# Moving the second gate, two shared-expert steps and one column copy in the last layer of a fused four-layer kernel

## The reference

```python
def _L3_ffn_ref(x, centroids, gate_bias, wg_s, wu_s, wd_s, wg, wu, wd):
    def _swiglu(x, wg, wu, wd):
        return jax.nn.silu(x @ wg) * (x @ wu) @ wd
    shared = _swiglu(x, wg_s, wu_s, wd_s) * RATIO
    affinity = jax.nn.sigmoid(jnp.einsum('bsh,eh->bse', x, centroids))
    _, top_idx = jax.lax.top_k(affinity + gate_bias, K)
    top_aff = jnp.take_along_axis(affinity, top_idx, axis=-1)
    weights = top_aff / (top_aff.sum(-1, keepdims=True) + EPS)
    mask = (jax.nn.one_hot(top_idx, E, dtype=x.dtype) * weights[..., None]).sum(-2)
    routed = jnp.zeros_like(x)
    for e in range(E):
        routed = routed + mask[..., e:e + 1] * _swiglu(x, wg[e], wu[e], wd[e])
    return shared + routed
...
x = x + _L3_xattn_ref(_layernorm(x, axis=-1), ctx_2048, ...)
x = x + _L3_ffn_ref(_layernorm(x, axis=-1), ...)
```

## Time and profile before

| | |
|---|---|
| median of three runs | 1159.66 us (1155.91 to 1160.9) |
| the profiled execution | 1160.9 us |
| its span in the trace | 1159.6 us |
| mean granted clock of TensorE | 0.914 of full speed |
| busy, share of the span | PE 85%, PEld 68%, DVE 66%, ACT 55%, POOL 45% |

### The profile page before, as it was taken

One profiled execution on the slowest core, in us unless ns is written; L12 is line 12 of the kernel. 1 busy time (PEld: TensorE's weight loads), 2 busy tenths in 40 slices (PEclk: granted clock), 3 DMA queues, 4 the chain that ended last, 5 costly groups with the idle time before them and its releaser, 6 DMA issues. The chain is left out here.

```text
span 1159.6 us, 17917 instructions
## 1 busy us (share of the span) xinstructions
PE 985.5 (85%) x5740; PEld 787.3 (68%) x5740; DVE 760.7 (66%) x2019; ACT 633.7 (55%) x1824; POOL 525.5 (45%) x582
## 2 busy tenths in 40 slices
PE   4957998187997964689999999999999889997897
PEld 2453555045585754578988888889899768676685
DVE  3766222275666428878888888887877588677544
ACT  1431444002124335779797879888888745463253
POOL 1441587243554343334545454544443236352453
PEclk8877999688997985779999999999999899998999
DMA  9130698920002764010101010101000025004584
GB/s 392 42 124 21 176 220 210 251 60 1 1 1 92 259 220 177 25 60 2 60 1 61 1 60 2 60 1 60 1 23 2 1 93 159 1 1 177 185 311 159
DMA packets 57261, 108.84 MB, mean 94 GB/s; under 512 B 13840, under 2 KB 35216, under 8 KB 55248
## 3 DMA queue, kind: packets, MB, share of 16 engines
q1 hardware_dynamic: 47920, 89.71, 23.3%
q0 software_dynamic: 9248, 18.00, 6.0%
HBM read 79.19 MB, written 27.42 MB: 92 GB/s over the span
## 5 line engine op out<-in xcount | busy, mean ns | idle before, releaser
L2919 POOL TENSOR_TENSOR a_p<-a_p,a_tot 128x128 f32<-128x128 f32 x64 | 51.0, 816 | 207.8 <-DVE a_tot L2531 207.8
L200 PE MATMUL bank<-a_w_high,a_in 128*128 128x128 f32 (+1 forms) x512 | 125.9, 287 | 5.3 <-DVE a_in L2131 4.5
L200 PE MATMUL bank<-a_w_low,a_in 128*128 128x128 f32 (+1 forms) x512 | 121.9, 284 | 0.0
L200 PEld LDWEIGHTS bank<-a_w_high,a_in 128*128 128x128 f32 x512 | 100.4, 196 | 7.5 <-issue 4.0
L200 PEld LDWEIGHTS bank<-a_w_low,a_in 128*128 128x128 f32 x512 | 100.5, 196 | 0.0
L2582 DVE TENSOR_REDUCE a_top<-bank 128x2 f32<-128x512 f32 (+1 forms) x96 | 56.9, 601 | 32.2 <-PE bank L2384 19.7
L2089 POOL DMA_INDIRECT f_ys<-f_y,f_got x54 | 51.8, 960 | 53.4 <-ACT f_y L2058 52.8
L2753 ACT ACTIVATE a_qn<-bank,a_q_shift,a_q_rstd 128x128 f32<-128x128 f32 x128 | 48.4, 461 | 42.0 <-POOL a_q_shift L256 42.0
L2560 DVE TENSOR_SCALAR a_qn<-bank,a_qk_minus,a_qk_rstd 128x128 f32<-128x128 f32 x192 | 64.1, 403 | 5.5 <-POOL a_qk_rstd L253 2.8
L2384 PE MATMUL bank<-a_kt,a_qt 128*128 128x256 f32 x256 | 67.1, 408 | 0.0
L200 PE MATMUL bank<-a_proj_high,a_catq 128*128 128x256 f32 x256 | 63.9, 288 | 1.0 <-issue 1.0
(11 more groups left out here) (424 smaller groups left out, 3016.9 us busy)
## 6 DMA issues: line engine op xcount, KB each, us to landing
expert<-in_experts SPq DMA_DIRECT2D x49, 384.0 KB, 4.4
f_expert<-in_experts SPq DMA_DIRECT2D x31, 384.0 KB, 6.2
third_shelf<-in_groups SPq DMA_DIRECT2D x8, 1024.0 KB, 6.5
f_got<-f_xs SPq DMA_DIRECT2D x10, 516.0 KB, 8.1
f_got<-f_ys SPq DMA_DIRECT2D x8, 512.0 KB, 5.1
third_shelf<-in_groups SPq DMA_DIRECT2D x8, 512.0 KB, 4.2
f_xs<-blank_zero SPq DMA_DIRECT2D x1, 3999.0 KB, 20.6
l_expert<-in_experts SPq DMA_DIRECT2D x10, 384.0 KB, 8.0
```

Source lines behind the costliest of these rows:

```text
L200: ins = pe.matmul(out, lhs, rhs, start=start and n == 0, stop=stop and n == len(pairs) - 1, skip_group_check=shared)
L2919: g_.tensor_tensor(cross_probs(m, ti), cross_probs(m, ti), over(m.tot[n % 2][:, first:first + HPG], SC), ALU.mult).then_inc(*s["cross_weig ...
```

## The change

It has four parts, all in the last layer.

1. `SPARSE3` takes 4 tiles of tokens through the shared experts ahead of the routed tiles where it took 5. So 8 of the 16 steps run ahead and 8 behind (10 and 6 before). `summed`, which says after how many additions a group of x is complete, is written for the new count.
2. On TensorE the gate's product of the second half is written ahead of the counts of the first half (`logits_tensor(k, p, s4, 1)` ahead of `ranks(0)`). For layer 1 this changes nothing, since `ranks(0)` stands further up there.
3. On VectorE the copy and the limit of the second half's logits are written ahead of the slots of the first half (`limit_vector` ahead of `slots_vector`).
4. In the attention the copy of the first half's columns moves from ahead of the addition of tile 6 to ahead of that of tile 7.

```diff
@@ -1487,12 +1487,11 @@
     def summed(self, n):
-        return self.early // self.shared + TOP * (n + 1) + (
-            0 if self.early == self.steps else NT - self.early // self.shared - (2 if n < GROUPS // 2 else 0))
+        return self.early // self.shared + TOP * (n + 1) + (0 if self.early == self.steps else HALF // 2 if n < GROUPS // 2 else HALF)
...
-SPARSE3 = Sparse("f3", 1 + E0 + 1 + E1, 2, E3, 0.1, "gate3", "bias3", 5)
+SPARSE3 = Sparse("f3", 1 + E0 + 1 + E1, 2, E3, 0.1, "gate3", "bias3", HALF)
@@ -1714,9 +1713,9 @@
     turn_half_tensor(k, s4, 1, m.rows, rows_of(s4))
+    logits_tensor(k, p, s4, 1)
     if not p.weighed_rows:
         ranks(0)
-    logits_tensor(k, p, s4, 1)
     for r in range(2):
         open_shared(r)
     ranks(1)
@@ -1927,8 +1926,8 @@
         choose_vector(k, p, m, s4, 0, facts)
         weights_vector(k, p, m, s4, 0)
+        limit_vector(k, p, m, s4, 1)
         slots_vector(k, p, m, s, 0)
-        limit_vector(k, p, m, s4, 1)
     choose_vector(k, p, m, s4, 1, facts)
@@ -3326,7 +3325,7 @@
             on.wait_ge(*s["x_biased"].at(i + 1))
-            if i == NT - 2:
+            if i == NT - 1:
                 half_cols_vector(k, s4, k.cols, 0)
             v.tensor_tensor(k.x[:, i, :], k.x[:, i, :], k.bank[6][:, 0:D], ALU.add).then_inc(*s["x_added"].one())
```

## The result

| | median (us) | range | runs |
|---|---|---|---|
| before | 1162.01 | 1155.44 to 1167.59 | 20 |
| after | 1172.03 | 1163.72 to 1179.02 | 20 |

The ratio is 1.0081 (95% interval 1.0059 to 1.0102), which is 9.4 us slower (6.9 to 11.9); the two medians lie 10.0 apart. The forecast was 1166.7, in 1161.5 to 1170.5, from an effect of 7.05: the sign is right, the time lies 1.5 us above the range. The profiled execution took 1170.14 with a span of 1168.8 (1159.6 before).

The account below looks back on a forecast made before the run. It took the chain from the first half's slots through the scatters and load to the routed tiles as the bound. 3.0 + 1.85 + 2.2 + 0 = 7.05 over the median 1159.66 gave 1166.7 us, range 1161.5 to 1170.5.

Parts of the forecast that it names:

- The first scatter, +3.0: Second gate product ahead of the first half's slots delays them and all sixteen scatters by 3.0 us (1.3 to 3.45).
- The restart, +1.85: Ahead of the routed tiles, TensorE's pause grows to 4.0, its clock falls, and the first tile takes 1.85 us more (0 to 3.7).
- VectorE's hold-up: In the early shared steps, VectorE, late with the second half's choice, holds them up by 2.2 us.
- The tail, +2.2: Behind the routed tiles, two moved shared steps make the first group's additions start 2.2 us later (1.8 to 2.8).
- The copy, 0: In the attention, moving the copy of the columns costs x 0 us; a wait for GpSimd covers the gate's 0.33 delay.
- held over the pause: Rival ahead of the routed tiles: TensorE's clock stays up, so 5.2 us slower, 1164.9; chance 0.14.
- came up during the product: Rival at the second gate product: clock up there, first term 1.3, whole 5.3 us, 1165.0; chance 0.16.
- The rival on the other side: Early shared steps, not loads, bound the routed tiles' start; kernel 1.2 us faster, 1158.5; chance 0.04.

Follow-up runs that it names:

- first pair: The first comparison's profiled executions of the unchanged kernels before and after the change; ratio 1.0081.
- e5_after_warm_gate: The kernel after plus four matmuls with unused results ahead of the turn-over of the second half's rows; one run, 1166.57 us.
- first kind: Chips, or a condition of one, where the kernel before runs at about 1161 us, without ScalarE's long waits.
- b_before: The kernel before, unchanged, profiled once more; before took 1161.12 us in that set of runs.
- a_after: The kernel after, unchanged, timed once more against the kernel before; ratio 1.0077.
- second kind: Chips, or a condition of one, where the kernel before runs at 1177 to 1182 us, with waits on ScalarE.
- q4: The kernel after plus four matmuls with unused results ahead of the second turn-over, timed against the kernel before; ratio 1.0019.
- second pair: The repeat of the unchanged kernels before and after, in another set of runs; ratio 1.0077.
- e7: The kernel before with only the gate's new order (parts 2 and 3), a repeat, against the kernel before; ratio 0.9986.
- e8: The kernel after plus twelve matmuls with unused results behind the early shared steps, a repeat, against the kernel before; ratio 1.0031.
- p1_before: The kernel before, unchanged, profiled beside other experiment kernels on one chip; one run, 1176.11 us, where before had 1181.05.

## Why the prediction was right or wrong

**The first scatter, +3.0: right.** 2.83 in the first pair; 2.6 in the second. The product started at 1063.36, 1.21 behind the forecast's 1062.15, about as much as x7 is late (1.32), and took 3.60 for 3.57. The scatters kept their pitch and didn't stop between the eighth and the ninth. How much of it is the lower clock, e5_after_warm_gate lets one estimate: its product was 1.35 shorter, and 2.83 - 1.35 = 1.5 is about the term's lower bound (1.3 with the clock up). Its whole 8.54 - 7.89 = 0.65 says less, since its turn-over ran faster than that of the kernel before too.

**The restart, +1.85: the step that failed, in size.** It measured 2.59 and 2.54. Two readings in it were off, and the first is the one that cost the time.

The price was taken from layer 1, with the words "such a pause was 2.01, and the granted clock then fell to 0.50", as if its 6.23 were a restart at the lower clock. It was one only in part. The stretches of layer 1's restart, which began at 385.03, in the trace of the kernel before:

```profile
385.00:387.00 2.00, 1.80 (x8) 1.08 (x8) 0.85 (x2) 0.00 (x0) 0.00 (x0) 1.00 0.94 260
387.00:389.00 2.00, 1.90 (x6) 1.50 (x6) 0.72 (x2) 0.28 (x1) 0.00 (x0) 0.50 1.04 333
```

The clock was still up behind the pause and fell only 2 us into the work. The first four matmuls on `f_cols` took 1.14 there, and 2.04 in the last layer after. The other four traces of the first kind show the same code of layer 1 with the clock down from the start. Their pauses there were 3.27 (b_before), 3.32 (a_after), 3.42 (after) and 3.42 (e5), and the way to the down product took 7.13, 6.99, 6.95 and 6.92. That is as much as the 6.97 and 7.07 behind the pauses of 5.97 and 5.78 in the last layer. By these rows (my estimate, 6.9 to 7.1 less the 4.4 of the trace before) the restart would have cost some 2.5 to 2.7 with the forecast's own pause of 4.0 too, and the length beyond that isn't what adds to it: 4.18 of pause in e5 went with only 6.38. What differs there is when the clock came back, 4.9 us behind the first `f_got` in e5 and 6.1 in after.

The second reading is the length of the pause. The step had the early steps "end at 1090.69 + 2.2 - 2.8 = 1090.1", hence a pause of 4.0. The loads came when I said (1095.53 less the 1.32 of x7's shift is 1094.2, against 1094.1), but the early part ended at 1088.33 + 1.23 = 1089.56, which less 1.32 is 1088.2, 1.9 too early. A wait for VectorE stands in the middle of the early steps, 2.52 long before and 2.58 after. TensorE before, timeline and stretch:

```profile
1079.67 0.33 PE L209 MATMUL bank<-const,f_swi_inner 128*128 128x128 f32 x1 [2.52 <-DVE f_swi_inner L1915]
...
1080.60 1.91 PE L200 MATMUL bank<-l_expert,cols 128*128 128x256 f32 x4
```

```profile
1080.00:1081.50 1.50, 1.50 (x5) 1.13 (x5) 0.14 (x1) 0.28 (x1) 0.96 (x1) 0.50 0.25 88
```

and after:

```profile
1083.03 0.33 PE L209 MATMUL bank<-const,f_swi_inner 128*128 128x128 f32 x1 [2.58 <-DVE f_swi_inner L1914]
...
1083.63 1.03 PE L200 MATMUL bank<-l_expert,cols 128*128 128x256 f32 x4
```

```profile
1083.00:1085.00 2.00, 1.97 (x10) 1.74 (x11) 0.50 (x2) 0.58 (x3) 1.48 (x2) 1.00 0.33 118
```

Before, the clock had fallen in that wait and the next four matmuls took 1.91; after, it held and they took 1.03. From the wait's end to the end of the part it is 11.0 before and 6.5 after: 2.8 for the two steps, and 1.7 for the clock. The remaining 0.2 are VectorE's hold-up, 2.0 instead of 2.2.

I had carried the slow matmuls over, but they go with the old order of the gate. b_before has them again (1.91 behind a wait of 2.52), and a_after doesn't (1.03 behind 2.59). From 26 to 27 us behind x7 the granted clock is 0.50 in all eight traces with the old order and 1.00 in eleven of the twelve with the new one, e5 being the exception. What lies ahead differs: with the old order TensorE waits 1.15, 1.83 and 2.52 in the early steps of the trace before, with the new one 3.20, 0.23 and 2.58 in the trace after. With the new order the clock falls behind the first of these waits (0.58 from 1074.18 to 1075.00) and is back ahead of the last. So this too is an effect of parts 2 and 3 that the prediction put at nothing. That it goes by the waits ahead is argued from their order, not shown by an experiment.

**The tail, +2.2: right.** 2.23 in the first pair, 57.83 against 55.60, and 1.9 to 2.2 wherever kernels with and without the moved steps stand beside each other in the table. The first group's additions follow the last shared product without a wait.

**The copy, 0: right on the first kind.** x7 moved by 0.12, and x7 to slots is the same with it (10.72) as for the gate's order alone (10.69 to 10.96, second kind).

**The rivals.** The clock neither held over the pause nor came up during the product. The Trainium skill (TensorE: Matmul & The Clock Gate, part 1, on what is actually happening) says that the point of transition varies, since what the gate looks at isn't tied to where the program begins. The runs agree that it varies: one kernel met its first gate product with the clock up in e5 (1.96) and falling in q4 (2.76). The rival on the other side had 0.04. On the first kind it was rightly small; on the second kind the routed tiles follow the early steps without a pause in every trace, and the place I named for it (early steps that end more than 3.0 later than in the trace) was the right one to watch.

**The time: outside the range, by the base more than by the restart.** The effect was 9.4 (6.9 to 11.9) against 7.05, which lies inside the interval, and the stretches give 7.9 and 7.0 for it. Each term of the sum came out inside its own bounds. The forecast of 1166.7 stood on a median of three runs, 1159.66; that of twenty is 1162.01. So 2.35 of the 5.3 that were missing are the base, 0.7 the restart, 0.2 the handover to the load (which had no term; in the second pair it was 0.3 shorter), 0.1 part 4, and the first term gives 0.1 back. The rest, some 2.0, is in nothing that the two traces show in the changed code. The range took in the spread of the runs with 0.9 at its upper end (1169.6 to 1170.5), less than the base alone was off. With the right base the same sum gives 1169.1, inside the range though still 3.0 short; with the restart right and the base as it was, it gives 1167.4.

**What stays open.** How the pause divides between the moved steps and the gate's order on a chip of the first kind: neither was run there alone. By the stretches, the gate's order alone would leave a pause of about 0.40 + 2.8 - 2.0 + 1.7 = 2.9 (1.7 for the clock, which goes with that order), and the steps alone 0.40 + 2.8 = 3.2. Either is near the pauses of layer 1 that went with the whole price of a restart, so each part alone might cost most of the 2.6 that they cost together; that is argued, not shown. Open is also what ScalarE waits for on the second kind, since the profile names no releaser, and whether the two kinds are really two chips.

## What to carry to other kernels

An instruction that waits holds back all that is queued behind it on its engine: look at what stands there before you move one forward, and if the wait is for small matmuls, price them at the clock they would run at. Work that covers a wait for a transfer isn't idle ballast: when it goes, TensorE pauses and the next tile pays for the clock as well, here 2.6 us for a pause of 6, and as much for one of 3.3 in layer 1. Before you take the price of a restart from another place, look at the clock in each microsecond of it: the 6.23 of layer 1 was a restart that began at full clock. And a slot that is full on one chip may have room on another: the same change was 0.8% slower in two comparisons and not slower in a third, where ScalarE stood still for microseconds and the early steps ended last.

## What the runs showed of the hardware

- The same kernel ran at 1161 to 1162 us in some sets of runs and at 1177 to 1182 in others. Part of it is ScalarE standing still at a gate activation (L1044): each of the 15 traces of the second kind has one such wait of 4.0 to 9.0 us, and none of the first kind's has one. In 13 of them it ended 2.6 to 3.7 us behind the start of the sixteenth scatter, in e7 and e8 2.8 us ahead of it. No semaphore of the profile explains it. The rest of the difference, 7 us at x7 in p1_before, is ahead of the change, where single gate activations of layer 0 (3.29) and layer 1 (4.00) come late in the same manner.
- A wait of 2.5 us at the same place of the program left TensorE's granted clock at 0.50 in both traces of the kernel before on the first kind, and at 1.00 in both of the kernel after. The length of a wait alone doesn't say whether the clock falls.
- Behind a pause of 2.01 the clock was still up and fell 2 us into the work (6.23 for the tile); behind pauses of 3.3 to 3.4 and of 5.8 to 6.0 it was at 0.50 from the start (6.9 to 7.1).
- Sixteen matmuls of 128x16 took 1.85 at a granted clock of 1.00 and 3.6 at 0.50, and 2.79 where it fell among them, with TensorE busy all the while.
